# Layer 0 of a four-layer kernel: how the stacked queries and keys of its attention are filled

## The reference: what is computed

```python
Q = layernorm(x) @ Wq + bq                       # 32 heads of 16 features
K = ctx @ Wk + bk; V = ctx @ Wv + bv             # 8 heads of 16, each shared by 4 query heads
scores = einsum('bhgqd,bhkd->bhgqk', Q, K) / 4   # per batch, float32
w = softmax(scores)                              # over the 128 keys
y = einsum('bhgqk,bhkd->bhgqd', w, V)
x = x + y @ Wo + bo
```

## Time and profile before

| | |
|---|---|
| median of 3 runs | 1290.59 us |
| the profiled execution, its own time | 1297.16 us |
| its span, from the first to the last instruction | 1295.9 us |
| granted TensorE clock, mean over the span | 0.977 |
| PE busy | 1212.4 us, 94% |
| DVE / ACT / POOL busy | 65% / 53% / 32% |
| layer 0 attention, first to last turned scores (L622) | 85.6 to 204.1 us |

### The profile page before, as it was taken

How to read it: one execution, slowest core, us unless ns; L and a number is a source line. 1 busy time by engine, 2 the same in 40 slices (tenths; PEclk the granted TensorE clock), 3 DMA queues, 4 the chain that set the end, 5 groups by cost and what they waited for, 6 DMA issues and landing times.

```text
span 1295.9 us, 16380 instructions
## 1 busy us (share of the span) xinstructions
PE 1212.4 (94%) x5860; PEld 946.8 (73%) x5860; DVE 836.0 (65%) x1547; ACT 690.2 (53%) x1575; POOL 415.8 (32%) x486
## 2 busy tenths in 40 slices
PE   4979887989999999989999999998999999999997
PEld 4756554656676676768888888877888888888765
DVE  5546665776776678475566666784446666667756
ACT  3235454337777778435555555672345555566621
POOL 5341120066777677101232223240022232323200
PEclk8979998999999999989999999999999999999998
DMA  7464430178667967622111121220302121211101
GB/s 246 146 200 111 143 119 33 40 266 271 106 125 198 265 146 145 165 88 65 58 58 65 44 63 47 60 82 26 96 26 65 58 65 58 65 42 49 57 1 65
DMA packets 73985, 130.49 MB, mean 101 GB/s; under 512 B 11376, under 2 KB 30704, under 8 KB 71344
## 3 DMA queue, kind: packets, MB, share of 16 engines
q1 hardware_dynamic: 55584, 80.91, 20.0%
q0 software_dynamic: 18320, 48.52, 15.1%
HBM read 150.37 MB, written 29.10 MB: 138 GB/s over the span
## 4 chain that ended last, share of the span: by engine, by line
PE 71%; DVE 10%; DMA 6%; issue 5%; POOL 4%; ACT 3%; SPq 0%; POOLq 0%; ACTq 0%; DVEq 0%
PE bank L451 54%; PE bank L1969 7%; PE bank L1945 4%; DMA moe<-ys,token_out 3%; POOL moe L1545 2%; PE bank L635 2%; DVE rden L841 1%; POOL xs L1534 1%; PE bank L2284 1%; DMA q0st<-m0T 1%; DVE xn L422 1%; PE bank L1221 1%; DVE stats L397 1%; PE bank L622 1%; PE bank L607 1%
## 5 line engine op out<-in xcount | busy, mean ns | idle before, releaser
L1937 POOL TENSOR_SCALAR p<-p,mx 128x256 f32<-128x256 f32 x256 | 162.8, 652 | 524.5 <-DVE mx L1931 524.5
L1130 DVE TENSOR_TENSOR wf_lo<-wf_raw,wf_hi 128x512 fp32r<-128x512 f32 x192 | 124.4, 689 | 37.6 <-ACT wf_hi L1124 33.0
L1923 ACT ACTIVATE p<-bank,mx 128x256 f32<-128x256 f32 x256 | 118.0, 485 | 10.7 <-DVE mx L1913 10.6
L451 PE MATMUL bank<-xnA_hi,w1q_hi 128*128 128x512 f32 x288 | 118.8, 412 | 3.6 <-DVE xnA_lo L445 3.2
L1124 ACT ACTIVATE wf_hi<-wf_raw 128x512 fp32r<-128x512 f32 x192 | 110.1, 625 | 11.5 <-DMA wf_raw<-in_wffn,weight_row 11.5
L451 PE MATMUL bank<-xnA_hi,w1q_lo 128*128 128x512 f32 x288 | 114.8, 399 | 0.0
L451 PE MATMUL bank<-xnA_lo,w1q_hi 128*128 128x512 f32 x288 | 114.2, 397 | 0.0
L1952 ACT ACTIVATE p1T_hi<-bank 128x512 fp32r<-128x512 f32 x128 | 75.1, 596 | 65.7 <-PE bank L1945 65.7
L1877 ACT ACTIVATE q1T_hi<-bank 128x512 fp32r<-128x512 f32 x64 | 38.2, 597 | 132.6 <-PE bank L451 132.6
L451 PE MATMUL bank<-w1o_hi,a1T_hi 128*128 128x512 f32 x256 | 105.2, 411 | 0.1
L451 PE MATMUL bank<-wf_raw,zT 128*128 128x512 f32 x220 | 102.9, 593 | 2.2 <-DVE x L1204 1.3
(11 more groups left out here) (337 smaller groups left out, 3129.3 us busy)
## 6 DMA issues: line engine op xcount, KB each, us to landing
w_raw<-in_wq SPq DMA_DIRECT2D x64, 256.0 KB
w_raw<-in_wo SPq DMA_DIRECT2D x64, 256.0 KB
q0st<-q_rows SPq DMA_DIRECT2D x8, 768.0 KB, 5.5
moe<-xn SPq DMA_DIRECT2D x2, 2304.0 KB, 14.0
q_rows<-q0T_hi SPq DMA_DIRECT2D x16, 256.0 KB
returned<-moe SPq DMA_DIRECT2D x8, 512.0 KB, 7.3
k0bd<-k_rows SPq DMA_DIRECT2D x16, 192.0 KB, 5.9
x<-in_x SPq DMA_DIRECT2D x8, 256.0 KB, 6.8
```

Source lines behind the costliest of these rows:

```text
L451: ins = nc.tensor.matmul(ps, a, b, start=(n == 0), stop=(n == len(pairs) - 1))
L1130: nc.vector.tensor_tensor(wf[m % 2][1][:, a, c, :], raw[m % STREAMS][:, a, c, :], wf[m % 2][0][:, a, c, :].bitcast(F32), ALU.subtract).the ...
L1923: ins = nc.scalar.activation(pr1[s % 2][:, h, :], banks.of(("s1", s, n))[:, hh * 2 * P:(hh + 1) * 2 * P], ACT.Exp, bias=m[:, UH + h:UH + h ...
L1937: ins = nc.gpsimd.tensor_scalar(pr1[s % 2][:, h, :], pr1[s % 2][:, h, :], m[:, 3 * UH + h:3 * UH + h + 1], 1.0, ALU.mult, ALU.mult)
```

## The change

The stacks are filled straight from SBUF (on-chip memory): `q_rows` and `k_rows` are gone. For one batch, the queries come as 12 transfers of 64 KB, one for each slice m and piece c, each from 128 partitions of `q0T` into 8 rows of `q0st` (`queries_in(b, m)`); the keys as 6 transfers of 64 KB, each into 16 rows (`keys_in`). The columns of the query weight and the key weight are permuted as they are copied (`query_weight`, and `wk`), so that the features fall in the right order. The maxima are issued by SP instead of POOL. There are now three `k0bd` and four `q0st` buffers. Queries, keys and values are computed as native float32 matmuls from operands that are not split, so the splitting on ACT, DVE and POOL is gone, and a group has 4 float32 matmuls instead of 12 of kind fp32r. ACT issues the first four tiles of x itself; SP loads the query weight first. The order of the opening is another: queries 0 and 1, keys, queries 2 and 3 first; the four query slices of the second half are moved into the loop, at steps -1, 3, 6 and 9. The gate's weights and the shared expert's 1.5 MB are brought in the round of b = 2. The zero fill of layer 1's buffers comes after all query pieces.

```diff
+        q0T = pair("q0T", [P, KT, HT])
+        qst23 = [sb(f"q0st{i}", [P, KV0, 2, P], F32R) for i in (2, 3)]
+        ctxT = [sb(f"ctx0_{i}", [P, KT, HT]) for i in range(2)]
+        wq = sb("wq0", [P, KT, D])
...
+        qst = [sb(f"q0st{i}", [P, KV0, 2, P], F32R) for i in range(2)] + qst23
         kbd.append(sb("k0bd2", [P, KV0, 2, P], F32R))
-        qst.append(sb("q0st2", [P, KV0, 2, P], F32R))
-        place[0] = kept
-        kbd.append(sb("k0bd3", [P, KV0, 2, P], F32R))
...
+        QUERY_STEPS = (-1, 3, 6, 9)
...
-            for b in range(HB):
-                load(x[:, b, :], A["x"][b]).then_inc(S[f"rows_in{b}"], 16)
-            load(w_raw[:, :, :], A["wq0"]).then_inc(S["ld_w0"], 16)
...
+            load(w_raw[:, :, :], A["wq0"]).then_inc(S["ld_wq0"], 16)
+            load(wkv[:, 0], A["wkv0"][:, 0]).then_inc(S["ld_wk0"], 16)
+            load(ctxT[0][:, :, :], A["ctxT"][0]).then_inc(S["ld_ctx00"], 16)
+            for m in range(KT):
+                first = HD0 * (m // 2) + HD0 // 2 * (m % 2)
+                load(bq[:, m:m + 1], A["bq0"].rearrange("(k p) n -> p n k", k=KT)[first:first + HD0 // 2],
+                     allow_slow_non_contiguous=True).then_inc(S["ld_bq0"], 16)
+            load(bk[:, :], A["bk0"].rearrange("(k d) o -> d k o", d=HD0),
+                 allow_slow_non_contiguous=True).then_inc(S["ld_bk0"], 16)
+            load(wkv[:, 1], A["wkv0"][:, 1]).then_inc(S["ld_wv0"], 16)
+            load(bv[:, :], A["bv0"].broadcast_to([P, P])).then_inc(S["ld_wv0"], 16)
+            sp.wait_ge(S["kones"], 2)
+            for s in range(1, KRING):
+                load(kbd[s][QROWS:QROWS + MROWS, :, :, :].bitcast(F32),
+                     kbd[0][QROWS:QROWS + MROWS, :, :, :].bitcast(F32)).then_inc(S[f"ld_k0{s}"], 16)
             for b in range(HB, B):
                 load(x[:, b, :], A["x"][b]).then_inc(S["ld_x_rest"], 16)
-            sp.wait_ge(S["ctx0_lo"], KT)
-            load(ctxT_raw[:, :, :], A["ctxT"][1]).then_inc(S["ld_ctx00"], 16)
-
...
-            def queries_out(half, m):
-                sp.wait_ge(S["q0_lo"], half * KT + m + 1)
-                for c in range(3):
-                    load(q_rows[half, 4 * m:4 * m + 4, :, c].rearrange("k h d t -> (k h) d t"),
-                         q0T[STACK_Q[c]][:, m, :].bitcast(F32)).then_inc(S["st_q"], 16)
...
+                sp.wait_ge(S["kbd_set"], b % KRING + 1)
+                sp.wait_ge(S["k0_lo"], half + 1)
                 if b >= KRING:
                     sp.wait_ge(S["t0_mm"], KV0 * (b - KRING + 1))
                 for h in range(2):
-                    load(kbd[b % KRING][QROWS // 2 * h:QROWS // 2 * (h + 1), :, h, :].bitcast(F32),
-                         k_rows[half].rearrange("k c d t -> (c d) k t")[:, :, tok]).then_inc(S[f"ld_k0{b % KRING}"], 16)
-
-            def queries_in(b):
+                    for c in range(3):
+                        row = QROWS // 2 * h + HD0 * c
+                        load(kbd[b % KRING][row:row + HD0, :, h, :].bitcast(F32),
+                             k0T[half][STACK_K[c]][:, tok].bitcast(F32)).then_inc(S[f"ld_k0{b % KRING}"], 16)
+
+            def queries_in(b, m):
                 half, tok = b // HB, slice((b % HB) * P, (b % HB + 1) * P)
-                sp.wait_ge(S["st_q"], 48 * KT * (half + 1))
+                sp.wait_ge(S["q0_lo"], half * KT + m + 1)
+                if b >= RING0:
+                    sp.wait_ge(S["t0_mm"], KV0 * (b - RING0 + 1))
+                for c in range(3):
+                    row = QROWS // 2 * (m // 2) + HD0 * c + HD0 // 2 * (m % 2)
+                    load(qst[b % RING0][row:row + HD0 // 2, :, :, :].bitcast(F32).rearrange("p k j t -> p (k j) t"),
+                         q0T[STACK_Q[c]][:, m, tok].bitcast(F32)).then_inc(S[f"ld_q0{b % RING0}"], 16)
+
+            def maxima(b):
+                half = H0 // 2
+                sp.wait_ge(S["m0_lo"], b + 1)
+                for q in range(2):
+                    for h in range(2):
+                        row = QROWS + 2 * q + h
+                        load(qst[b % RING0][row:row + 1, :, :, :].bitcast(F32).rearrange("p k j t -> p (k j) t"),
+                             mT[b % 2][h * half:(h + 1) * half, q, :].bitcast(F32)).then_inc(
+                                 S[f"ld_m0{b % RING0}"], 16)
+
+            for m in range(KT):
+                if m == 2:
+                    keys_in(0)
+                    queries_in(3, 0)
+                for b in range(3):
+                    queries_in(b, m)
+            keys_in(1)
+            keys_in(2)
+            maxima(0)
+            for m in range(1, KT):
+                queries_in(3, m)
+            for b in range(1, B):
+                maxima(b)
+                if b + 2 < B:
+                    keys_in(b + 2)
+                if b + 3 < B:
+                    for m in range(KT):
+                        queries_in(b + 3, m)
                 if b == 2:
                     sp.wait_ge(S["wo0_lo"], KT)
-                if b >= RING0:
-                    sp.wait_ge(S["t0_mm"], KV0 * (b - RING0 + 1))
-                load(qst[b % RING0][0:QROWS, :, :, :].bitcast(F32).rearrange("p k j t -> p (k j) t"),
-                     q_rows[half].rearrange("k h c d t -> (h c d) k t")[:, :, tok]).then_inc(S[f"ld_q0{b % RING0}"], 16)
...
+        def opening_steps(i, turn, values, keys, query, maxima):
             j = i + LEAD_S
-            if j < KV0 and j % 4 == 3:
-                query(KT // 2 + j // 4)
+            if j in (1, 2):
+                turn(j + 1)
             if j == KV0 - 1:
                 maxima()
+            if HB <= j < B:
+                values(j)
+            if j == KV0 + 1:
+                keys()
+            if i in QUERY_STEPS:
+                query(QUERY_STEPS.index(i))
...
+            def keys(half, n):
+                ps = banks.take(n, ("k0", half), (S["k0_lo"], half + 1))
+                pe.wait_ge(S["wk0"], 1)
+                pe.wait_ge(S[f"ld_ctx0{half}"], 16)
+                mm_group(ps[:, :], [(wk[:, k, :], ctxT[half][:, k, :])
+                                    for k in range(KT)]).then_inc(S["k0_mm"], 1)
...
-            def query(half, m, ring):
-                ps = banks.take(next(ring), ("q0", half, m), (S["q0_lo"], half * KT + m + 1))
-                pe.wait_ge(S["xn_lo"], HB * (half + 1))
-                pe.wait_ge(S["wq0_lo"], KT)
-                cols = slice(m * P, (m + 1) * P)
-                mm_group(ps[:, :], [q for k in range(KT) for q in three(
-                    (wq[0][:, k, cols], wq[1][:, k, cols]),
-                    (xnA[0][:, k, :], xnA[1][:, k, :]))]).then_inc(S["q0_mm"], 1)
+                mm_group(ps[:, 0:P], [(ctxT[b // HB][:, k, cols], wkv[:, 1, k, :])
+                                      for k in range(KT)]).then_inc(S["v0_mm"], 1)
+
+            def query(half, m, n):
+                ps = banks.take(n, ("q0", half, m), (S["q0_lo"], half * KT + m + 1))
+                pe.wait_ge(S["xn_ready"], HB * (half + 1))
+                pe.wait_ge(S["wq0"], KT)
+                mm_group(ps[:, :], [(wq[:, k, m * P:(m + 1) * P], xnF[half][:, k, :])
+                                    for k in range(KT)]).then_inc(S["q0_mm"], 1)
...
+            for k in range(HB):
+                norm_turn(0, k, k)
+            query(0, 0, 4)
+            query(0, 1, 5)
+            keys(0, 7)
+            query(0, 2, 0)
+            query(0, 3, 1)
+            norm_turn(1, 0, 2)
+            norm_turn(1, 1, 3)
+            for b, n in enumerate((4, 5, 7, 2)):
+                values(b, n)
             for i in range(-LEAD_S, UNITS0 + LAG_Y + 1):
                 if i + LEAD_S < UNITS0:
                     scores(i + LEAD_S)
                 if 0 <= i + LEAD_T < UNITS0:
                     turned_scores(i + LEAD_T)
...
                 if half:
-                    act.wait_ge(S["st_q"], 48 * KT)
+                    for b in range(HB):
+                        act.wait_ge(S[f"ld_q0{b}"], 192)
                 nc.scalar.activation(q0T[0][:, m, :], banks.of(("q0", half, m))[:, :], ACT.Identity,
                                      bias=bq[:, m:m + 1]).then_inc(S["q_hi"], 1)
 
+            def query_weight(k):
+                act.wait_ge(S["ld_wq0"], 16)
+                nc.scalar.activation(wq[:, k, :].rearrange("p (h d g) -> p h d g", h=2, d=HD0),
+                                     w_raw[:, k, :].rearrange("p (g h d) -> p h d g", h=2, d=HD0),
+                                     ACT.Copy).then_inc(S["wq0"], 1)
...
+            for b in range(HB):
+                nc.scalar.dma_start(x[:, b, :], A["x"][b]).then_inc(S[f"rows_in{b}"], 16)
+            norm_sqrt(0)
+            query_weight(0)
+            query_weight(1)
+            norm_hi(0, 0)
+            norm_hi(0, 1)
+            query_weight(2)
+            norm_hi(0, 2)
+            query_weight(3)
+            norm_hi(0, 3)
...
-                pool.wait_ge(S["m0_lo"], b + 1)
-                half = H0 // 2
```

(19 more changed lines are left out.)

301 lines of the change are left out of this document (89 added, 212 removed).

## The result

The changed kernel takes 1300.43 us (median of 5 runs, 1297.97 to 1303.75) against 1290.59 us of the kernel before (1289.38 to 1292.98): a ratio of 1.0072, interval 1.0056 to 1.0087. It is slower by 9.8 us, where 9 us less were forecast. The profiled execution has a span of 1299.1 us.

The account below looks back on a forecast made before the run. The opening was taken as a chain of dependent work with no engine full, everything later hanging on the attention's end. Batch 7's turned scores 9.0 us earlier (180.6 against 189.56) gave 1282 us; range for 8 in 10, 1274 to 1314.

Parts of the forecast that it names:

- q: SP's cost for one 64 KB query piece: 0.70 us taken, near the issue of 0.64, bounds 0.60 to 1.22.
- T0: Start of batch 0's turned scores, after 39 query pieces, 18 key pieces (k = 0.62 each) and maxima: 65.5 us, against 85.62.
- S: Time at which the first query slice is ready to be sent, after the opening: 23 us.
- rival 2: Pieces are bound where they land, in 8 partitions: q = 1.22, T7 = 220, +31 us, 1321 us; chance 0.22.
- rival 1: A piece is slower, q = 0.9 (0.8 to 1.05): T7 = 194.6, +5 us, 1296 us; chance 0.18.
- T2: Start of batch 2's turned scores, after four float32 query groups in the loop: T0 + 36.1 = 101.6 us, against 107.90.
- T3: Start of batch 3's turned scores, its maxima behind keys, queries and the 1.5 MB: T2 + 19.4 = 121.0 us, against 123.00.
- T7: Start of batch 7's turned scores, the mark by which the change was priced: 180.6 us, against 189.56.
- ACT's wait at q0T_hi: Before overwriting q0T at step -1, ACT waits for first-half pieces until T0 + 6.5; PE wants its exponentials at T0 + 8.8.
- Batches 4 to 7: Rounds from T3 to T7: SP's 14.3 us lies below PE's 15.1, so 15.1 three times and 14.3 last.
- Rival 3: The 1.5 MB do not hold up the maxima and q is 0.60: T7 = 174.6, -15 us, 1276 us; chance 0.10.
- Rival 4: PE stays at 1.2 GHz with query groups of 6.8 us: T0 = 68.2, 1285 us; chance 0.50 together with the forecast.

Follow-up runs that it names:

- e3: Changed kernel with the stack rows interleaved, so a piece's rows stand 2 apart, pieces otherwise unchanged: 1289.02 us, ratio 0.9982 to the kernel before.
- e10: Changed kernel with interleaved stack rows and ACT issuing nine query pieces beside SP: 1287.18 us, ratio 0.9959 to the kernel before.
- e5: Changed kernel with SP issuing the four tiles of x ahead of the weights and ACT's root table loaded early: 1294.53 us, ratio 1.0012 to before.
- e1: Changed kernel with the gate's weights and the 1.5 MB issued behind the maxima of batch 3 instead of ahead: 1295.81 us, ratio 1.0035 to before.
- e6: Changed kernel with the edits of e3 and e1 together: 1284.58 us, ratio 0.9947 to the kernel before.
- e9: Changed kernel with ACT issuing nine query pieces beside SP, rows left as they are: 1298.17 us, ratio 1.0047 to the kernel before.
- e2: Changed kernel with queries cut by head, so a 64 KB piece goes to 16 neighbouring rows: 1292.19 us, ratio 0.9999 to the kernel before.

## Why the prediction was wrong

**The step that failed is the cost of a piece.** The prediction took "half of the 16 engines" and 0.52 us for the landing from the share of 0.53 in the stores, so that the issue (0.64) came out the longer, and q = 0.70. The issue was right (0.65 with the gap). The landing was 0.92 on average up to the first scores. By T0, S + 39 q + 18 k + 4.0, this term with the landing of the maxima was to be 42.5 us (65.5 less 23); it was 50.8 (77.2 less 26.4), and 41.9 in e3, where the rows are spread. The stores went to DRAM, the loads of 254 GB/s into 48 and 96 rows; no row had shown 8 neighbouring rows. The range given for q (0.60 to 1.22) held it, and rival 2 named the mechanism; I put it at 0.22 for its extreme price and missed that it holds in part. The range of 1274 to 1314 us held the measured time by way of rivals 1 and 2; the forecast itself had the direction wrong.

The working behind the 0.52 does not hold either. The stores of the earlier trace rows and the loads beside them don't have the same runs: from 44 to 54 us the stores moved 1.97 MB in 1020 packets, some 2 KB each, against the 512 bytes of loads and pieces. And a share that reaches 1.24 is not a count of engines: pieces with the same 8 rows show 0.63 and 0.36 here. The 127 GB/s that "half of the engines" was to give is no limit: e10 moved 139 GB/s from 44 to 52 us, nearly all in such pieces. So 0.53 was no confirmation of the 8 engines.

**The path to T0 was another one too.** The forecast let SP's row of 57 issues gate the maxima of batch 0. In e3 it does: the maxima follow directly on the last key piece, at 64.51. In the changed kernel SP is done at 67.49 and then waits for the maxima, since the first scores had come so late:

```profile
SPq L516 <- DVE m0T L824: 4.7, 1, 4.7
```

**Term by term** (us; forecast of the likeliest case, of rival 1 with q = 0.9, measured, and e3, whose pieces are not bound at the rows):

| | forecast | rival 1 | measured | e3 |
|---|---|---|---|---|
| S, first piece issued | 23 | 23 | 26.4 | 26.5 |
| T0 | 65.5 | 73.3 | 77.2 | 68.4 |
| T2 | 101.6 | 110.0 | 114.5 | 104.7 |
| T3 | 121.0 | 131.8 | 135.7 | 124.8 |
| T7 | 180.6 | 194.6 | 198.4 | 187.6 |

The measured column is rival 1's, later by 3.8 to 4.5 us, of which S is 3.4. That it fits so well is luck in part: rival 1 too had SP's row gate T0, and SP's longer rounds stretch the batches behind T3. e3 is the forecast's, later by 3 to 4 up to T3 and by 7 at the end. So the 17.8 us between 180.6 and 198.4 are, in these executions: 10.8 the landing (e3), 3.4 the start, and 3.6 the later batches.

- **S, 3.4 us late.** "All there at about 7.4 us": the last tile of x was read at 12.01, as ACT's and SP's loads share the engines (in e5, where the tiles come first, it is read at 7.00). ACT's table (1.28) was not in the sum; the strided copies took 1.06 to 1.08 us each, not 0.6, as the text had allowed. My 6 us for the first query group were 3.7 in this execution. The other kernels with this opening had up to 29.5 for S, so 3.4 is near the least of it.
- **T2 = T0 + 36.1**: measured 37.3. The four groups took 3.43 to 3.45 each. Right.
- **ACT's wait at q0T_hi**: "covered by 1 us only; at q = 0.9 it is not". It waited 4.4 us for pieces of L507. Right.
- **T3 = T2 + 19.4**: measured 21.2. The maxima wait behind the 1.5 MB and land 6.85 us after their issue; e1 prices the order of the loads at 4.6 us for the whole. The prediction had a wait of about 4 us here, measured 6.73.
- **Batches 4 to 7, 59.4 us**: measured 62.7, and 62.7 in e3. Rival 1 has 62.8 too, but by SP's longer rounds, and these can't be it, since e3 has none. What the trace shows: PE waits for maxima at three of the four batches, 0.60, 1.29 and 1.51 us, much as before, where the forecast had taken these waits as gone. And after the wait of 6.73 us the first matmuls are slower: the first value product takes 1.71 us instead of 0.86 (the granted clock of 135 to 145 us is 0.80), so batch 4 comes at +16.4. But in e1 and e6, whose waits at batch 3 are 1.36 and 0.61 us, it comes at +16.2 and +16.3, with the new wait at the scores in place of the slow clock. So this term was not taken apart, and its cause stays open. The chain of the changed kernel behind that wait:

```profile
136.43 1.71 PE bank L643 x2
...
140.44 0.86 PE bank L643 x2
```

- **Rival 3** (the 1.5 MB cost nothing) is refuted by e1. **Rival 4** (groups of 6.8 us) is refuted by the 3.43 for all groups but the first: in e9 PE needs 9.32 us for 14 recorded matmuls of the first two groups, where the changed kernel needs 7.13 for 16, and S is 29.5.

**Why slower than before, not only less fast than forecast.** At T0 the change is ahead by 8.4 us. It then pays 13.8 for four float32 groups in the loop. The kernel before had its queries behind it at that point, and the changed one had let 19 us pass in which PE stood idle. With 1.2 us more in between this makes it 6.6 us late at batch 2. The prediction had this in its sum, with 20 us of lead to pay from; at a lead of 8.4 it turns the sign. The round with the 1.5 MB costs another 6.1 (21.2 us to batch 3 against 15.1), and 3.8 of it come back, since the kernel before pays for its own loads and maxima behind batch 3 (66.6 us to batch 7 against 62.7).

## What to carry to other kernels

Price a transfer by its landing where its destination differs from every row at hand: look at how many neighbouring partitions one piece fills, and interleave the rows of a stack if they are few; here that took only other row numbers and was worth 11 us. A busy share of the transfer engines is not their work: the same pieces showed 0.63 at 76 to 84 GB/s into one set of rows and 0.36 at 100 into another. A count of engines can't be read from it either. Work put into a loop should be weighed against the gap that the same change opens ahead of it. And a start that scatters by 3 us is not judged from one execution.

## What the runs showed of the hardware

Copies of 64 KB within the on-chip memory, in runs of 512 bytes, landed at 76 to 84 GB/s into 8 neighbouring partitions, whether one queue (the changed kernel, 44 to 58 us) or two issued them (e9, 42 to 52 us). Into 8 partitions with a step of 2, or into 16 neighbouring ones, they landed at 99 to 106, the rate of the issues (e3, e2). With two issuers and a step of 2 they reached 177 in 2 us and 139 over the 8 behind (e10). The transfer engines were 0.63 busy in the changed kernel and 0.36 in e3, which differs from it in the rows alone, so a busy share contains waiting at the destination. Issues of such a copy took SP 0.61 us, 0.65 from one to the next.

A native float32 matmul of 512 columns took 0.86 us in a group of four at a granted clock of 1.00 (3.43 for the group). The first such groups after the start took 7.13 us for 16 recorded matmuls in some executions and 8.8 and more in others of the same opening.
